# A long convolution's transform at half samples, and new orders of all turns, in a four-layer kernel

## The reference

```python
# layer A: long convolution
q, k, v = (x @ W.T + b for ...)               # then a 3-tap causal convolution of q and k
kv   = k * v
kv_f = rfft(kv, n=512);  h_f = rfft(ssm_kernel, n=512)   # along the 256 positions
y    = irfft(kv_f * h_f, n=512)[..., :256]
y    = (y + kv * D_skip) * q;   return y @ Wo.T + bo
# layer B: rms norm, 16-head causal attention used as a modulation of a gated MLP (width 1024)
# layer D: q * cumsum(k * v) * c, projected
# layer F: router over 64 experts (6 chosen), shared expert, expert MLPs (width 176)
```

## Time and profile before

| | us |
|---|---|
| median of 3 runs | 1036.09 (1034.62 to 1038.6) |
| span of the profiled execution | 1034.5 |
| fill and turn 0, to 41.9 | 41.9 |
| turn 1 | 77.4 |
| one of turns 2 to 7 | 77.3 to 77.4 |
| last turns and routing, 583 to 703 | 119.6 |
| experts, 703 to 984 | 281.0 |
| sum and norm of the 16 tiles | 50.5 |

### The profile page before, as it was taken

How to read it: one execution, slowest core, us unless ns; L and a number is a source line. 1 busy time by engine, 2 the same in 40 slices (tenths; PEclk the granted TensorE clock), 3 DMA queues, 4 the chain that set the end, 5 groups by cost and what they waited for, 6 DMA issues and landing times. The chain is left out here.

```text
span 1034.5 us, 20988 instructions
## 1 busy us (share of the span) xinstructions
PE 967.6 (94%) x6481; PEld 799.2 (77%) x6481; DVE 608.1 (59%) x2176; ACT 338.7 (33%) x1038; POOL 456.8 (44%) x516
## 2 busy tenths in 40 slices
PE   7988999999999999999999899868999999999986
PEld 6766887877877877877887677647888888888865
DVE  4745466676676676666676546644555555555266
ACT  1244263264264264263263362101111111111243
POOL 1132152283283283283283371541566656656622
PEclk9999999999999999999999999888999999999999
DMA  9597790510510510510510510159869697878296
GB/s 360 192 277 136 203 263 10 133 38 23 137 37 21 137 37 21 137 38 20 128 43 17 129 52 11 64 211 317 335 205 351 211 311 232 295 229 304 85 347 219
DMA packets 103271, 163.28 MB, mean 158 GB/s; under 512 B 26961, under 2 KB 77106, under 8 KB 101042
## 3 DMA queue, kind: packets, MB, share of 16 engines
q1 hardware_dynamic: 85746, 113.31, 37.9%
q0 software_dynamic: 12288, 33.96, 8.7%
q10 hardware_dynamic: 5184, 15.36, 4.1%
HBM read 139.32 MB, written 61.87 MB: 194 GB/s over the span
## 5 line engine op out<-in xcount | busy, mean ns | idle before, releaser
L1282 ACT ACTIVATE prob<-bank,nmx 128x128 f32<-128x128 f32 (+1 forms) x256 | 104.9, 432 | 63.5 <-DVE nmx L1587 63.4
L641 POOL TENSOR_TENSOR prob<-prob,rec 128x512 f32<-128x512 f32 x96 | 99.3, 1041 | 40.8 <-DVE rec L1593 40.0
L673 POOL DMA_INDIRECT x_rows<-x_copy,desti x84 | 85.8, 1021 | 18.3 <-issue 18.3
L1587 DVE TENSOR_REDUCE nmx<-bank 128x2 f32<-128x512 f32 (+1 forms) x96 | 65.1, 685 | 46.6 <-PE bank L889 45.9
L1275 ACT ACTIVATE probT<-bank 128x512 f32<-128x512 f32 x96 | 58.0, 604 | 56.6 <-PE bank L749 55.8
L749 PE MATMUL bank<-cst,prob 128*128 128x128 f32 x384 | 60.6, 282 | 10.3 <-POOL prob L641 6.0
L663 POOL TENSOR_TENSOR products<-z,products 128x512 bf16<-128x512 f32 x8 | 9.2, 1155 | 136.6 <-ACT products L1263 136.6
L949 PE MATMUL bank<-h2T,w_up 128*128 128x256 f32 x256 | 66.4, 382 | 0.0
L951 PE MATMUL bank<-h2T,w_in 128*128 128x256 f32 x256 | 65.7, 379 | 0.0
L749 PEld LDWEIGHTS bank<-cst,prob 128*128 128x128 f32 x384 | 44.4, 145 | 20.2 <-POOL prob L641 10.1
L1282 ACT ACTIVATION_READ_ACCUMULATOR prob<-bank,nmx 128x1 f32 x256 | 55.8, 218 | 0.0
(11 more groups left out here) (445 smaller groups left out, 2500.9 us busy)
## 6 DMA issues: line engine op xcount, KB each, us to landing
w_in<-in_e_w SPq DMA_DIRECT2D x20, 448.0 KB
w_up<-in_e_w SPq DMA_DIRECT2D x20, 448.0 KB
w_down<-in_e_w SPq DMA_DIRECT2D x20, 448.0 KB
products<-in_e_w SPq DMA_DIRECT2D x20, 448.0 KB
prob<-in_e_w SPq DMA_DIRECT2D x20, 448.0 KB
probT<-in_e_w SPq DMA_DIRECT2D x20, 448.0 KB
actT<-in_e_w SPq DMA_DIRECT2D x20, 448.0 KB
x_rows<-sgt SPq DMA_DIRECT2D x1, 8320.0 KB, 28.9
```

The lines of the kernel that those rows point to most:

```text
L641: pool.tensor_tensor(p, p, r, ALU.mult).then_inc(S["b_scaled"], 1)
L673: pool.indirect_dma_start(x_rows, bass.IndirectOffsetOnAxis(ap=desti[:, n:n + 1].bitcast(U32), axis=0), rows[:, n // TOPK, :], None).then_ ...
L1282: i = act.activation(prob[:, u % PROBS, h * w:(h + 1) * w], psum(u % 2, h * w, (h + 1) * w), ACT.Exp, bias=nmx[:, u, h:h + 1], accum_out=s ...
L1587: dve.tensor_reduce(nmx[:, u, 0:512 // w], bank[:, u % 2, :].rearrange("p (h k) -> p h k", k=w), AX, ALU.max, negate=True).then_inc(S["b_m ...
```

## The change

The 256 positions are folded about their middle: early half plus reversed late half, and early half minus reversed late half. With cosines and sines at half samples, (2t+1)f, each of even and odd frequencies needs one of the two folded halves, so each product contracts over 128 positions, not 256. The kernel's own spectrum is still made from full tables (`long`, 24 instructions as before, 128 KB smaller). What is different:

- Tables: `fwd` and `inv` become `long`, `fold`, `unfold`. The order of loads is the same but for `fold`, with a semaphore of its own, before `a_wq`.
- New part `Zf` on POOL: two operations of 256 elements (sum, difference, one operand read backwards) write `folded`, which lies in k_sb's place. `Z2` transposes folded and waits for it.
- `A3a`/`A3b` have two products each, with one contraction tile. `A4a`/`A4b` have four products of 128 columns each; even part to bank 4, odd part to bank 5, both for all channels after A4b.
- `A4y` on DVE is now the whole step: copy of the odd part (into kv's place), difference and sum in the banks, two products with qc, the second one written backwards. `A4z` is gone.
- `Z1k` on ACT waits for the transposes of Z2 of the batch before, not for the convolution.
- New orders in all turns for all engines. On PE in "turn": A3a is ahead of u0, A3b ahead of D1, and D1 u1 u2 follow with nothing between; A4a and A4b are together behind D3; C1 is behind SDb; C2 is behind f4; Z1k is between f6 and f7. On DVE, D5h is last before B8, and D3n, A5n, A5o, A6n and A6o move. On POOL the scatters are spread to the second half of the turn, G11 stands behind Zf, and D6 behind B8. In "second", u0 is ahead of A3a. In "last_but_one", D1 is ahead of u0. In "last", S2 is behind DTb on PE and H7 behind ED_0 on POOL.

```diff
-        fwd, inv = sb("fwd", [P, KT, 6 * P]), sb("inv", [P, 2 * FREQ_TILES, L])
+        long = sb("long", [P, KT, 5 * P])
+        fold, unfold = sb("fold", [P, 4, P]), sb("unfold", [P, 4, P])
...
+        folded, behind = k_sb[:, :, 2:], kv[:, :, 0:P]
...
             "second": {
-                "pe": """A2 A3a A3b u0 u1 u2 u3 u4 A4a A4b u5 u6 A5 u7 u8 u9 u10 u11 u12 u13 u14 u15 B6c B6b C1 f0 f1 C2 f2 f3 f4 f5 C2v f6 Z1k f7 Z1v Z1q B8 Z2""",
+                "pe": """A2 u0 A3a u1 A3b u2 u3 A4a A4b u4 u5 A5 u6 u7 u8 u9 u10 u11 u12 u13 u14 C1 u15 B6c B6b C2 f0 f1 f2 f3 f4 C2v f5 Z1k f6 f7 Z1v Z1q B8 Z2""",
...
             "turn": {
-                "pe": """u0 A3a u1 D1 A3b u2 D2k u3 D2x u4 D2q A4a u5 D3 u6 A4b u7 u8 A5 D4 u9 u10 S0 u11 S1 D4l u12 S2 u13 u14 SDa u15 B6c B6b C1 SDb f0 f1 f2 C2 D5 f3 C2v
-                        f4 f5 f6 f7 Z1k Z1v Z1q B8 Z2""",
...
-                "dve": """u0 u1 u2 A3p u3 u4 D2v D2w u5 u6 D3n A4y u7 A4z D3o u8 u9 A5n u10 S0 A5o u11 A6n S1 D4m u12 A6o S2 B6b D4t SD C1 f0 D4k f1 f2 D5p C2 f3 f4 D4w D5h f5
-                        f6 Zk f7 Zq B8""",
-                "pool": """G0 u1 u2 G1 A3p u3 u4 G2 G3 G4 u5 u6 G5 D3n u7 G6 u8 G7 G8 A5n u9 u10 G9 G10 u11 A6n u12 C2v G11 D6 C2h B8""",
+                "pe": """A3a u0 A3b D1 u1 u2 D2k u3 D2x u4 D2q u5 D3 A4a A4b u6 u7 u8 A5 D4 u9 u10 S0 u11 S1 u12 D4l S2 u13 u14 SDa u15 B6c B6b SDb C1 f0 f1 f2 f3 f4
+                        C2 D5 f5 C2v f6 Z1k f7 Z1v Z1q B8 Z2""",
...
+                "dve": """u0 u1 u2 A3p u3 D2v u4 D2w u5 D3n u6 A4y u7 D3o u8 u9 u10 A5n S0 u11 u12 S1 D4m A5o S2 A6n A6o B6b D4t f0 SD C1 f1 D4k f2 C2 D5p D4w f3 f4
+                        f5 f6 f7 Zk Zq D5h B8""",
+                "pool": """G0 u1 u2 G1 u3 A3p u4 G2 u5 u6 D3n u7 G3 u8 G4 u9 G5 A5n u10 u11 u12 G6 A6n G7 G8 C2v G9 G10 C2h Zf G11 B8 D6""",
             },
             "last_but_one": {
-                "pe": """u0 u1 D1 u2 u3 D2k D2x u4 D2q u5 u6 D3 u7 u8 u9 D4 u10 S0 u11 S1 u12 D4l S2 u13 u14 SDa SDb u15 B6c B6b f0 f1 f2 f3 f4 D5 f5 f6 f7 L8""",
...
+                "pe": """D1 u0 u1 D2k D2x u2 D2q u3 D3 u4 u5 u6 u7 D4 u8 S0 u9 u10 S1 u11 D4l u12 S2 u13 u14 SDa u15 B6c B6b SDb f0 f1 f2 f3 D5 f4 f5 f6 f7 L8""",
...
+            def Zf(b):
+                pool.wait_ge(S["a_kv"], b + 1)
+                need(pool, "a_kvT", b)
+                early, late = kv[:, :, 0:P], kv[:, :, L - 1:P - 1:-1]
+                pool.tensor_tensor(folded[:, :, 0:P], early, late, ALU.add).then_inc(S["a_fold"], 1)
+                pool.tensor_tensor(folded[:, :, P:L], early, late, ALU.subtract).then_inc(S["a_fold"], 1)
...
-                pe.wait_ge(S["a_kv"], b + 1)
+                pe.wait_ge(S["a_fold"], b * 2 + 2)
...
-                    for n in range(part * FREQ_TILES, (part + 1) * FREQ_TILES):
-                        for kt in range(KT):
-                            mm = pe.matmul(psum(4 + part, (n % 2) * D, (n % 2 + 1) * D), fwd[:, kt, n * P:(n + 1) * P],
-                                           kvT[:, kt, :], start=(kt == 0), stop=(kt == KT - 1))
+                    if first(b):
+                        pe.wait_ge(S["ld_fold"], 16)
+                    for n in range(FREQ_TILES):
+                        mm = pe.matmul(psum(4 + part, n * D, (n + 1) * D), fold[:, part * FREQ_TILES + n, :],
+                                       kvT[:, (n + part) % 2, :], start=True, stop=True)
...
+                    for i, y in enumerate((Yre, Yim)):
+                        if dh == 0:
+                            pe.wait_ge(S["a_Y"], b * 2 + 1 + i)
+                        for n in range(FREQ_TILES):
+                            side = (n + i) % 2
+                            mm = pe.matmul(psum(4 + side, dh * P, (dh + 1) * P), y[:, n, dh * P:(dh + 1) * P],
+                                           unfold[:, i * FREQ_TILES + n, :], start=(i == 0), stop=(i == 1))
...
+                dve.wait_ge(S["a_y"], b * 2 + 2)
+                even, odd = halves_of(4), halves_of(5)
+                dve.tensor_copy(behind, odd).then_inc(S["a_ab"], 1)
+                dve.wait_ge(S["a_ab"], b * 3 + 1)
+                dve.tensor_tensor(odd, even, behind, ALU.subtract).then_inc(S["a_ab"], 1)
+                dve.tensor_tensor(even, even, behind, ALU.add).then_inc(S["a_ab"], 1)
+                dve.wait_ge(S["a_ab"], b * 3 + 3)
+                dve.tensor_tensor(z[:, :, 0:P], even, qc[:, :, 0:P], ALU.mult).then_inc(S["a_z"], 1)
+                dve.tensor_tensor(z[:, :, L - 1:P - 1:-1], odd, qc[:, :, L - 1:P - 1:-1], ALU.mult).then_inc(S["a_z"], 1)
```

More of the change, by code:

```diff
@@ L111, in constants, with angle, half_angle @@
     t = np.arange(L)[:, None]
[L112 to L126, removed]
+    even, odd = 2 * p[None, :], 2 * p[None, :] + 1
+    packed = np.where(even == 0, L, even)
+    def angle(f):
+        return 2 * np.pi * ((t * f) % NFFT) / NFFT
+    long = np.concatenate([np.cos(angle(even)), np.cos(angle(odd)), -np.sin(angle(even)), -np.sin(angle(odd)), np.cos(angle(packed))], 1)
+    long[:, 2 * P] = 0
+    long[:, 4 * P + 1:] = long[:, 1:P]
+    long = long.reshape(KT, P, 5 * P).transpose(1, 0, 2)
+    def half_angle(f):
+        return np.pi * (((2 * t[0:P] + 1) * f) % (2 * NFFT)) / NFFT
+    fold = np.stack([np.cos(half_angle(even)), np.cos(half_angle(odd)), -np.sin(half_angle(packed)), -np.sin(half_angle(odd))], 1)
+    weight = np.full((P, 4, 1), 2.0 / NFFT)
+    weight[0, 0], weight[0, 2] = 1.0 / NFFT, 1.0 / NFFT
+    unfold = weight * fold.transpose(2, 1, 0)
     return {
         "blank": blank, "cst": c, "csb": b.astype(mybir.dt.np(BF16)),
-        "fwd": np.ascontiguousarray(fwd, np.float32), "inv": np.ascontiguousarray(inv, np.float32),
+        "long": np.ascontiguousarray(long, np.float32), "fold": np.ascontiguousarray(fold, np.float32),
+        "unfold": np.ascontiguousarray(unfold, np.float32),
     }
@@ L246, in build @@
         cn, cum, pad_e = scr[:, 3], scr[:, 4], scr[:, 5]
-        dead = [[t[:].rearrange("p a b -> p (a b)"), 0] for t in (w_in, w_up, w_down, fwd, inv, products.rearrange("p n f d -> p (n f) d"),
+        dead = [[t[:].rearrange("p a b -> p (a b)"), 0] for t in (w_in, w_up, w_down, long, fold, unfold, products.rearrange("p n f d -> p (n f) d"),
                                                                  prob[:].rearrange("p n (a b) -> p (n a) b", a=4), probT[:].rearrange("p n j q -> p (n j) q"), actT,
@@ L486, in _ @@
             sp.dma_start(a_w["k"][:], d["a_wk"]).then_inc(S["ld_ak"], 16)
-            sp.dma_start(fwd[:], d["fwd"]).then_inc(S["ld_ssm"], 16)
+            sp.dma_start(long[:], d["long"]).then_inc(S["ld_ssm"], 16)
             sp.dma_start(ssm[:], d["ssm"]).then_inc(S["ld_ssm"], 16)
             sp.dma_start(mixed[0:1, :], d["skip"]).then_inc(S["ld_ssm"], 16)
+            sp.dma_start(fold[:], d["fold"]).then_inc(S["ld_fold"], 16)
             sp.dma_start(a_w["q"][:], d["a_wq"]).then_inc(S["ld_aq"], 16)
@@ L700, in scatter @@
                 return part
-            turns(pool, "pool", {"A3p": A3, "C2v": C2v, "C2h": C2h, "D6": D6, "D3n": inverse_root("D"), "A5n": inverse_root("A"), "A6n": inverse_root("R"),
+            turns(pool, "pool", {"A3p": A3, "Zf": Zf, "C2v": C2v, "C2h": C2h, "D6": D6, "D3n": inverse_root("D"), "A5n": inverse_root("A"), "A6n": inverse_root("R"),
                          "B8": inverse_root("B"), **{f"{g}{n}": scatter(n) for n in range(TT * TOPK) for g in "GH"},
@@ L792, in A2 @@
                     pe.wait_ge(S["set_skip"], 1)
-                    for n, tile0, tile1 in ((0, 0, 1), (1, 4, 3), (2, 5, 1)):
+                    for n, tile0, tile1 in ((0, 0, 1), (1, 2, 3), (2, 4, 1)):
                         for ft, m in enumerate((tile0, tile1)):
                             for kt in range(KT):
-                                mm = pe.matmul(psum(n, ft * D, (ft + 1) * D), fwd[:, kt, m * P:(m + 1) * P], ssm[:, kt, :],
+                                mm = pe.matmul(psum(n, ft * D, (ft + 1) * D), long[:, kt, m * P:(m + 1) * P], ssm[:, kt, :],
                                                start=(kt == 0), stop=(kt == KT - 1))
                         mm.then_inc(S["set_pe"], 1)
-                pe.wait_ge(S["a_kv"], b + 1)
+                pe.wait_ge(S["a_fold"], b * 2 + 2)
                 pe.wait_ge(S["a_k_out" if first(b) else "a_q_out"], b + 1)
-                turn_tiles(psum(5), kv).then_inc(S["a_kvT"], 1)
+                turn_tiles(psum(5), folded).then_inc(S["a_kvT"], 1)
             def forward(part):
@@ L819, in A4 @@
                         pe.wait_ge(S["ld_b"], 128)
[L820 to L823, removed]
-                        mm = pe.matmul(psum(4 + dh, 0, L), y[:, n % FREQ_TILES, dh * P:(dh + 1) * P],
-                                       inv[:, n, :], start=(n == 0), stop=(n == 2 * FREQ_TILES - 1))
+                    for i, y in enumerate((Yre, Yim)):
[5 more added lines that the diff above has]
```

(1 more changed line is left out.)

37 lines of the change are left out of this document (16 added, 21 removed), and 20 rows, old and new, of the table ORDER.

## The result

The changed kernel takes 1032.5 us against 1037.1 us for the kernel before on the same chip: a ratio of 0.9946, 95% interval 0.9925 to 0.9966. The forecast was 1016.5 with a range from 1006 to 1028, so about a quarter of the forecast gain of 19.6 us arrived. One of the changed kernel's ten executions took 1906 us, for a reason that nothing here shows, and is left out of the ratio. The profiled execution spans 1030.3 us (1034.5 before).

The account below looks back on a forecast made before the run. PE's own work, busy 94% of the span, was taken as the bound. First two turns 5.0, turn 2 2.6, five turns of 2.6 - 0.8, tail 3.0: 19.6 off 1036.1 gives 1016.5 us, range 1006 to 1028.

Parts of the forecast that it names:

- PE's saving: Forward and inverse transforms on PE: 1.73 us less each, 3.46 per turn, 27.7 over eight turns.
- u2 to A5: Middle of a steady turn on PE: 17.97 us falls to 16.24 plus 0.15 of waiting, gain 1.6 per turn.
- The sum set against it: Inverse transform: if weight loads cannot overlap, at least 3.0 us, returning 14 us less; left out of the forecast.
- PE's f6 meets it within 0.1 us: MLP: DVE's f3 stands behind C2 and D5p, yet PE's f6 would wait at most 0.1 us.
- The top of the turn: From Z2's transposes to u2: the forward transform's 1.73 us becomes waiting on kvT, x and ACT; gain only 0.1.
- POOL's scatters: Units 9 to 12: moving five scatters out returns 0.9 of the 1.0 us PE loses to POOL each turn.
- A5: PE's wait for DVE's longer A4: 0.15 us with u6 to u8 in between, 2.2 without that cover.
- G11 before B8: Scatter that D5h awaits ahead of B8: costs 0.8 us, of 0 to 2.5, in each of turns 3 to 7.
- rival (b): G11 lands as late as today: 5 x 1.7 us more, 1025, with a slow Zf 1027; chance 0.15.
- the tail's 3.0: Tail, with D1 first and D2k, D2x before u2: 3.0 us gained, of 0 to 5.
- The first turns: First and second turn: 5.0 us gained by the second's end, of 3 to 6; Zf costs 1.4, u0 starts at 55.1.
- Rival (d): Attention's chain sets the pace between u2 and u12, only the ends gain: about 1033, range 1028 to 1040; chance 0.1.

Follow-up runs that it names:

- the repaired orders: Changed kernel with f3, D5p and D5 ahead of C2, and G9 to G11, D6 and D5h back in the MLP: ratios 0.9790 and, on another chip, 0.9756 (1011.2 us).

## Why the prediction was wrong

**PE's saving**: right in kind and a little too large. The inverse's sixteen products take 1.79 from their start to the next group's (371.38 to 373.17), where 1.73 was counted, and u2 to A5 takes 16.45 (360.37 to 376.82), where 16.4 with 0.15 of waiting was forecast. By the busy column a turn saves 2.9 in the changed kernel and 3.3 under the repaired orders, of 3.46 counted. The sum set against it, with a bound of 3.0 us for the inverse, was off: 3.04 less 1.73 is 1.3 per turn and 10.5 over eight, not 14.

**"PE's f6 meets it within 0.1 us"**: the step that failed, 9.8 us over six turns. I saw that f3 stood behind C2 and D5p on DVE and gave D5p its 0.41. With 0.41, f3's activation ends near 335.6 and f6's own start, 335.78, meets it as forecast; with 2.29 it ends at 337.4. The exclusion of DVE and POOL was in my text, but only for Zf, where slack hid it. I asked it of the one new POOL instruction, and not of the pairs that the new orders put side by side.

**The top of the turn**: forecast 0.1 gained, measured 0.9 lost (u2 at t + 6.58, not 5.5; 5.68 before). D6 was moved behind B8, beside the norm (0.74, by the run that moved D6 alone), and DVE came to B8 0.2 late: D5h now fills DVE's time ahead of it, and Zf had stretched Zq before that by 0.75 (its six operations took 3.28, 2.53 in the kernel before). I never costed D6's move. The work was priced too low as well: 5.1 less 1.73 is 3.4, not 3.1, and with D6 moved u2 still stands at t + 5.81.

**POOL's scatters**: 0.9 forecast, and its waits are gone. **A5**: 0.15 of waiting forecast, none seen. But the run with the old orders shows what the cover was worth: 1.5 at A5 and 1.5 at S2, more than the 2.2 that I gave.

**G11 before B8**: a term of the wrong shape. I spread 0.8 over five turns, up to 2.5 each. In turns 3 to 6 D5h waited for nothing, and rival (b) was false there; in turn 7, where no Z parts stand between, it waited 5.74. With the clock's fall behind it that turned the tail's 3.0 into -0.9. With G9 to G11 early, the tail gained 4.5.

**The first turns**: 3.84 of 5.0. The wait for the fold is 2.41, 1.4 more than the 1.02 before, as forecast. A4 came 1.55 earlier, and A5 1.8 instead of 2.5. Behind the wait the fill products took 4.9 instead of 3.5, at a lowered clock. That alone is 1.4, and of two executions of the repaired kernel with the same wait, one shows it and one does not; there u0 starts at the 55.1 that I gave, but by luck in part: that execution was 1.0 ahead before it came to the wait.

**The clock** was in no term. In the changed kernel it costs 1.5 in turn six, 2.6 behind turn 7 (5.7 from D1 to D2v, 3.1 where the clock held) and 1.4 in the first turns. The kernel before pays a part of the second too, in its own fall from 592.0 to 595.2.

Worked back, against the forecast: f6 9.8, the top of five turns 5 x 1.0, the tail 3.9, the clock in turn six 1.5, the first turns 1.2; less the 4.0 kept for G11 and 1.6 that came behind the experts' start. That is 15.8, and the table's gains are 15.4 short of 19.6. Rival (d), whose 1033 comes nearest (its own terms, 19.6 less 6 x 2.5, give 1031.5), is not the cause: its mechanism, attention's chain between u2 and u12, shows no wait, and once the orders were mended the turn fell to 74.9, where 74.8 (77.4 - 2.6) was forecast without a DMA effect. By place the division came too: against the earlier trace rows the top lost 0.1 (0.1 gained was forecast), u2 to A5 gained 1.5 (1.6) and the rest of the turn 1.1 (0.9). By cause it can't be divided: the repaired orders bring the old transform 0.1 and the new one 4.6, and the new transform gains 2.5 in them and loses 2.0 in the old ones.

What stays open: why the granted clock falls after some idle stretches and not after equal ones, and why the experts' part differs by 55 us between chips.

## What to carry to other kernels

When an order is rewritten, list for every moved instruction what will run beside it on the other engine of a shared port, and give each such pair the longer of the two durations; here a 0.2 us DVE operation ahead of a critical one took 1.1. A DMA whose landing gates a critical step belongs in a quiet stretch, and the last turn, where other work no longer covers it, has to be costed by itself. Work with loose ends on both sides (here C2v, worth 1.8 us per turn) is a good filler for the waits that a shortened engine uncovers.

## What the runs showed of the hardware

- Beside a GpSimd instruction of 1.05 to 1.15 us, DVE operations with their operands in SBUF were held for up to its whole length: 64 elements bf16 with two operands took 1.17 instead of 0.18, a 256-element norm write with one tensor operand 1.29 instead of 0.41. Beside the fold's instructions of 0.72 to 0.83 us, Zq's first pair took 1.14 in a steady turn and 1.53 in turn 0 instead of 0.73. Operations with an operand in PSUM kept their time (0.42 at 575.87 in the changed kernel, beside POOL's 1.03 from 575.57).
- In an idle stretch of 7.5 us PE's granted clock fell to 0.50 and stayed there for 10 us, 5 of them at work. With one of 3.7 us it fell in one execution and not in another, and after three waits of about 1 us within 6 us it fell in one steady turn of four, in two executions in the same one. A fall cost 1.4 to 3 us.
- A scatter issued inside the stack transfers landed after 8.2 us.
